# Second attention of a fused transformer kernel: GpSimd subtracts the row maxima for two of four head groups, ScalarE makes one wide exponential of each, and the instruction sequences of all engines are new

## The reference

```
x = x + cross_attention_0(layernorm(x), ctx)   # 16 heads of 8, causal, bf16 projections
x = x + ffn_0(layernorm(x))                    # shared expert + top-1 of 8 experts
x = x + cross_attention_1(layernorm(x), ctx, bias)   # 16 heads of 8, fp32, softmax over 128 keys
x = x + switchhead(layernorm(x))               # 8 heads; gated sums over 8 experts for values and outputs
```

## Time and profile before

| what | value |
|---|---|
| time, median of 3 runs | 1476.98 us (1474.19 to 1478.59) |
| time of the profiled execution | 1472.34 us |
| its span, first to last instruction | 1470.6 us |
| TensorE matmul busy | 1380.0 us, 94% |
| TensorE weight load busy | 931.6 us, 63% |
| VectorE busy | 1293.0 us, 88% |
| ScalarE busy | 1256.4 us, 85% |
| GpSimd busy | 863.4 us, 59% |

### The profile page before, as it was taken

The page is one execution under the profiler, slowest core; times in us unless marked ns, Lnnn a source line. Parts: engine busy times, 40 slices in busy tenths (PEclk is TensorE's granted clock), DMA queues, the critical chain, the costliest instruction groups (busy, mean ns, idle before and its releaser), DMA issues. The chain is left out here.

```text
span 1470.6 us, 34271 instructions
## 1 busy us (share of the span) xinstructions
PE 1380.0 (94%) x9428; PEld 931.6 (63%) x9585; DVE 1293.0 (88%) x5266; ACT 1256.4 (85%) x4426; POOL 863.4 (59%) x1345
## 2 busy tenths in 40 slices
PE   3477999999999999999999999999999999999998
PEld 2255666666666666666666666666666666666654
DVE  3666989999999999999989999999999999999886
ACT  2666889999888899998889999888999988899886
POOL 2122665665666566666665665656566566655567
PEclk8688999999999999999999999999999999999999
DMA  4520010000111100011110000111000011100000
GB/s 119 166 76 25 26 28 24 18 20 26 29 29 29 29 16 23 21 28 28 29 29 17 22 21 28 29 29 28 22 18 22 26 29 29 29 23 7 21 3 4
DMA packets 99966, 44.97 MB, mean 31 GB/s; under 512 B 21248, under 2 KB 99776, under 8 KB 99776
## 3 DMA queue, kind: packets, MB, share of 16 engines
q1 hardware_dynamic: 82560, 34.13, 8.3%
q10 hardware_dynamic: 17216, 8.65, 2.1%
HBM read 25.70 MB, written 8.52 MB: 23 GB/s over the span
## 5 line engine op out<-in xcount | busy, mean ns | idle before, releaser
L3422 POOL TENSOR_TENSOR accO<-accO,TE 128x512 f32<-128x512 f32 x192 | 247.2, 1287 | 184.6 <-DVE TE L2514 172.3
L1365 ACT ACTIVATE TE<-psC,gateO 128x128 f32<-128x128 f32 x1024 | 290.9, 369 | 46.0 <-PE psC L325 35.3
L1365 ACT ACTIVATE TE<-psC,gate 128x128 f32<-128x128 f32 x1024 | 298.8, 402 | 12.3 <-PE psC L325 6.8
L2514 DVE SCALAR_TENSOR_TENSOR TE<-psC,gateO,TE 128x128 f32<-128x128 f32 x1024 | 282.3, 340 | 12.0 <-PE psC L325 10.6
L2514 DVE SCALAR_TENSOR_TENSOR TE<-psC,gate,TE 128x128 f32<-128x128 f32 x1024 | 284.0, 339 | 9.0 <-ACT TE L1365 4.3
L325 PE MATMUL psC<-Oh,ch 128*128 128x512 f32 x512 | 269.5, 526 | 4.7 <-DVE TE L2514 4.2
L325 PE MATMUL psC<-Vh,xTh 128*128 128x512 f32 x512 | 267.0, 521 | 2.6 <-ACT PTC L1365 1.0
L3410 POOL TENSOR_TENSOR TE<-TE 128x256 f32<-128x256 f32 x256 | 192.1, 750 | 123.6 <-DVE TE L2514 120.3
L325 PE MATMUL psC<-Vh,xTl 128*128 128x512 f32 x512 | 202.0, 395 | 0.0
L325 PE MATMUL psC<-Oh,cl 128*128 128x512 f32 x512 | 201.8, 394 | 0.0
L325 PE MATMUL psC<-Ol,cb 128*128 128x512 bf16 x478 | 186.2, 390 | 0.0
(11 more groups left out here) (229 smaller groups left out, 3318.4 us busy)
## 6 DMA issues: line engine op xcount, KB each, us to landing
bdB<-k_rows SPq DMA_DIRECT2D x128, 64.0 KB, 2.3
k_rows<-Kc SPq DMA_DIRECT2D x96, 64.0 KB, 2.0
Qs<-Qc SPq DMA_DIRECT2D x96, 64.0 KB, 1.9
raw<-in_L_ffn_v_w ACTq DMA_DIRECT2D x8, 512.0 KB, 4.0
raw<-in_L_ffn_o_w ACTq DMA_DIRECT2D x8, 512.0 KB, 3.9
x_sb<-in_x SPq DMA_DIRECT2D x32, 64.0 KB, 2.1
ctx_sb<-in_ctx SPq DMA_DIRECT2D x32, 64.0 KB, 2.0
bias_sb<-in_mask_Bx1xSxS_ff SPq DMA_DIRECT2D x32, 64.0 KB, 1.9
```

The lines of the kernel that those rows point to most:

```text
L1365: return A.activation(o, i, func, **kw)
L2514: m = V.scalar_tensor_tensor(TE[:, i, e], psC[:, p, e * P:(e + 1) * P], gates[:, e:e + 1], TE[:, i, e], ALU.mult, ALU.add)
L3422: G.tensor_tensor(accO[:], TE[:, slot(b, H1)] if h == 1 else accO[:], TE[:, slot(b, H1 + h)], ALU.add).then_inc(o_fe, 1)
```

## The change

For head groups 2 and 3 of stage B the subtraction of the maximum leaves ScalarE. A new GpSimd step `b_below(b, t)` waits for `b_nm`, computes `nmB - PTB` for the 128x512 of the group in one TENSOR_TENSOR, with `nmB` read with a stride of zero along the keys, and counts the new semaphore `b_sub`. ScalarE's `b_exp` then waits for `b_sub` and makes one ACTIVATE of 128x512 with no bias. Groups 0 and 1 stay as they were.

```diff
@@ ScalarE @@
             def b_exp(b, t):
                 if b not in BATCHES:
                     return
-                act.wait_ge(b_nm, 4 * b + t + 1)
-                for j in range(NJ):
-                    m = copy(PTB[:, t, j], PTB[:, t, j], ACT.Exp, bias=nmB[:, t, j:j + 1], scale=-1.0)
-                m.then_inc(b_e, 1)
+                if t < 2:
+                    act.wait_ge(b_nm, 4 * b + t + 1)
+                    for j in range(NJ):
+                        m = copy(PTB[:, t, j], PTB[:, t, j], ACT.Exp, bias=nmB[:, t, j:j + 1], scale=-1.0)
+                    m.then_inc(b_e, 1)
+                    return
+                act.wait_ge(b_sub, 2 * b + t - 1)
+                copy(flat(PTB[:, t]), flat(PTB[:, t]), ACT.Exp).then_inc(b_e, 1)
@@ GpSimd @@
+            def b_below(b, t):
+                if b not in BATCHES:
+                    return
+                pool.wait_ge(b_nm, 4 * b + t + 1)
+                G.tensor_tensor(PTB[:, t], along(nmB[:, t, :], P), PTB[:, t], ALU.subtract).then_inc(b_sub, 1)
@@ GpSimd, period @@
...
+                outputs(i - 7, 6)
+                b_below(i - 4, 2)
+                b_below(i - 4, 3)
+                outputs(i - 7, 7)
...
```

More of the change, by code:

```diff
@@ L2534, in start @@
             def start():
+                ones()
                 a_stats(0, 0)
@@ L2714, in start @@
                 b_bias(2, 2)
+                c_choice(1, 0)
                 b_bias(2, 3)
@@ L2765, in start @@
                 a_top(3, 1)
+                c_share(1, 4)
                 a_top(3, 2)
@@ L2789, in start @@
                 outputs(0, 5)
+                c_share(1, 6)
                 a_max(4, 0)
                 b_bias(3, 0)
-                a_max(4, 1)
                 outputs(0, 6)
@@ L2871, in start @@
                 outputs(1, 3)
-                c_share(2, 5)
+                outputs(1, 4)
+                b_queries(4)
                 c_norm(3)
-                outputs(1, 4)
                 c_share(2, 6)
-                b_queries(4)
+                a_max(5, 0)
                 outputs(1, 5)
@@ L2964, in start @@
                 b_bias(5, 0)
-                a_max(6, 0)
                 outputs(2, 6)
@@ L2968, in start @@
                 b_bias(5, 2)
+                a_max(6, 0)
                 a_max(6, 1)
-                a_stats(7, 0)
+                c_xl_(4)
                 b_bias(5, 3)
-                c_xl_(4)
                 a_max(6, 2)
                 a_max(6, 3)
+                a_maxt(6, 0)
                 c_weights(3, 0)
-                a_maxt(6, 0)
                 a_maxt(6, 1)
                 outputs(2, 7)
+                c_choice(4, 0)
                 a_withmax(6)
@@ L3054, in period @@
                 b_bias(i - 1, 0)
+                a_max(i, 0)
                 outputs(i - 4, 6)
@@ L3057, in period @@
                 b_bias(i - 1, 2)
-                a_max(i, 0)
                 a_max(i, 1)
+                c_xl_(i - 2)
                 b_bias(i - 1, 3)
-                c_xl_(i - 2)
+                c_choice(i - 2, 0)
                 a_max(i, 2)
@@ L3457, in start @@
                 b_root(0)
-                a_masks(2)
+                b_below(0, 2)
+                b_below(0, 3)
                 a_causal(1, 0)
@@ L3470, in start @@
                 a_root(3)
-                a_masks(3)
+                b_below(1, 2)
+                b_below(1, 3)
                 a_causal(2, 0)
@@ L3657, in end @@
                 c_gates(B - 4, 2)
+                outputs(B - 5, 6)
+                b_below(B - 2, 2)
+                b_below(B - 2, 3)
                 outputs(B - 5, 7)
                 a_causal(B - 1, 0)
-                result(B - 5, 0)
                 a_causal(B - 1, 1)
                 a_causal(B - 1, 2)
+                result(B - 5, 0)
                 a_causal(B - 1, 3)
```

1170 lines of the change are left out of this document (585 added, 585 removed).

## The result

The change takes 1459.51 us, median of 4 runs (1457.87 to 1463.57), beside 1476.96 us (1474.19 to 1478.59) for the kernel before. The ratio is 0.9895, with a 95% interval of 0.9881 to 0.9909: faster by 1.05%, inside the range of the prediction and 4.5 us above its 1455. Timed beside each other a second time, the two kernels stood at 1460.36 and 1473.83, 13.5 us apart where the first pair has 17.5. The profiled execution took 1457.87 us, its span is 1456.1.

What follows compares the result with a forecast made beforehand. It took a nearly full TensorE to bound the long middle. Terms of 0.3 + 0.4 + 0.1 = 0.8 us, times 28 repetitions, gave 22.4 us off 1472.3, with 4.6 added for the median: 1455 us, range 1432 to 1490.

Steps and rivals of the forecast that it cites:

- the least: TensorE's matmul row: its idle time, 0.52 us a repetition, as the lower figure for what a perfect change could take.
- the most that a perfect change could take: TensorE's queue: the weight loads' waits for VectorE and ScalarE results, 2.0 us a repetition.
- five named waits: TensorE's weight loads, six repetitions: VectorE's `TE` 3.0 us, ScalarE's `PTA` 2.5, `PTB` 2.2, `TE` 2.0, VectorE's `nmA` 2.2.
- about a quarter: Share of the weight-load waits (2.0 us a repetition) that the matmul row shows as idle time (0.52).
- part 2: VectorE's order: one `c_share` product moves, an `outputs` group starts sooner, TensorE's wait there goes; 0.4 us, ends 0.26 and 0.5.
- Part 1: ScalarE's exponentials: wide ones save 1.3 us of its queue, of which TensorE gains 0.3 us a repetition, ends 0 and 1.1.
- the 0.1 us of `a_max`: VectorE: `a_max(b, 0)` goes ahead of `outputs(b, 6)`, easing the wait for `nmA`; 0.1 us a repetition, ends 0 and 0.37.
- Part 3: GpSimd: two added 128x512 instructions, 2.6 us a repetition, fit into 4.60 us idle before `outputs` 7; cost nothing.
- Part 4: The rest: SyncE's new order changes nothing at a DMA share of 0.09; start and end nothing, 5 us either way.
- A: All of TensorE's named waits go, 1.4 to 2.0 us a repetition: 1429 us; chance 0.12.
- B: No change: savings given back at stage B's first scores, behind the `Qs` transfer, or wide exponentials wait for GpSimd; 1477, chance 0.15.
- C: Slower: GpSimd's second `b_below` locks out small VectorE instructions, 1.29 us per repetition against 0.8 gained: 1491; chance 0.20.

Runs made afterwards that it cites:

- less_pe: The change without the product of low x by high y in stage C's scores, two matmuls per element: 1447.12 us, ratio 0.9814 to before.
- share_only: The kernel before with one VectorE instruction moved, `c_share` 5 from behind `outputs` 4 to ahead of `b_norm`: 1473.88 us, ratio 0.9991 to before.
- seq_only: The change with its new lists, but small exponentials for all four groups and no `b_below`: 1486.91 us, ratio 1.0085 to before.
- math_only: The kernel before with `b_below` and the wide exponentials alone, the order of calls otherwise as it was: 1480.51 us, ratio 1.0043 to before.
- math_steady: The kernel before with `b_below` and wide exponentials only for elements 3 to 27: 1473.51 us, ratio 0.9996 to before.
- sp_slack: The change with SyncE's next masks, bias and store issued before stage A's keys: 1454.10 us, ratio 0.9867 to before; timed again 1455.28, 0.9872.
- pool_more: The change with a third 128x512 TENSOR_TENSOR on GpSimd behind the second `b_below`: 1477.71 us, ratio 1.0021 to before.

## Why the prediction was right, and where it was not

**The bound.** That the middle decides and that TensorE is nearly full was right; less_pe shows it directly. The 0.70 us spacing of the earlier trace rows, and not the share of the weight loads, was the right reading. By the rule that the prediction gives from the Trainium skill, Perfetto Trace Analysis, Identifying the Most-Contended Engine, VectorE at 93% would have been the bound. Here the runs say otherwise: share_only freed VectorE of 1.0 us of it for 0.03, and less_pe freed TensorE of 0.46 for 0.45.

**The step that failed: from waits to time.** The prediction called the matmul row's 0.52 us "the least" and the weight-load waits' 2.0 us "the most that a perfect change could take". What was gained, 0.45 us, lies at the least. The change removed four of the five named waits, (3.0 + 2.5 + 2.2 + 2.2)/6 = 1.65 us a repetition, but the weight loads wait only 0.5 us less in all, since most of it came back at other places; that is close to the 0.45 gained. The working had a conversion (about a quarter) and used it for two terms, but not for part 2, which took 0.4 whole; with it part 2 is 0.12 and the sum 0.52, which gives about 1462 us for the whole. The idle time of the row was the better estimate, but no strict ceiling: seq_only's row has 0.37 us idle, and the change runs 0.8 us shorter than it with the same list on TensorE.

**Part 1, ScalarE, 0.3 us.** Mis-sized: 0.14 to 0.17 alone (math_only, math_steady). The exponential came as forecast, 0.52 us against 1.17; ScalarE ended at 37.49 busy, for 37.0.

**Part 2, VectorE's order, 0.4 us.** Fell as a separate term: 0.03 alone. The stretch of the small products that it wanted removed was removed. The rows of L2474, which answer to L2469 of the earlier trace rows:

```profile
L2474 DVE TENSOR_TENSOR best<-best,gsum x46: 161/175/644, 329.7 to 1266.5; 128x16 f32<-128x16 f32 x46
```

The median fell from 401 to 175 ns, and the wait of TensorE for VectorE's `TE` from 3.0 us in six to 0.7 in 24 repetitions. But what pays is the whole of the lists together with the wide exponential (0.31), not this move alone; the 0.1 us of `a_max` had no run of its own, and its wait for `nmA` is gone.

**Part 3, GpSimd, nothing.** Right. `b_below` was cheaper than its nearest row, 1.04 against 1.285 us, and ended 0.71 us ahead of ScalarE for group 2, where 0.24 was allowed for. A third instruction there (pool_more) costs 18 us, so the cost of nothing holds for two and not for GpSimd as such.

**Part 4, SyncE, nothing.** Wrong by about 5 us, by sp_slack beside the change. I read the share of the DMA engines (0.09) and not SyncE's own queue: each issue takes 0.6 us of it, and with them in a row the last `Qs` issue has no slack. Start and end were put at "nothing, and 5 us either way"; they came out 6.5 us better in one execution and 4.2 in another at the head, and 0.7 at the tail, at or beyond the edge of that.

So the 22.4 us forecast for the middle were 7.3, a third. The head and tail, at which the forecast put nothing, gave 7.2, and the profiled execution of before lay 4.6 us below its median where that of the change lay 1.6 below: that the total came out 17.5 us, near the forecast, was in good part luck. Of the signs named, the repetition of 41.7 us did not come (42.05), and the sign of being wrong, TensorE's waits again under other names, came in part.

**The rivals.** A (1429) did not come: its 1.4 to 2.0 us a repetition were three times what the row had idle, and the next wait was there, as its own counter-argument said. B named its place well: the long repetitions end at the first scores and `Qs`. C's mechanism is real at the place named (pool_more), and the change misses it by 0.25 us.

## What to carry to other kernels

Take the idle time of the matmul row (0.52 us here, for 0.45 gained), not the sum of named waits on the weight loads (2.0), as the first estimate of what a reordering can give TensorE, and check the sum of the terms against it. It is an estimate and no bound, as seq_only shows. Once TensorE is full, the next microseconds are in the tail of the distribution: compare repetitions one by one, and give the transfer that TensorE needs first an idle SyncE ahead of it. When engine A is relieved and queues are in fixed order, the gain appears only with an order written for the new times: test both halves alone before crediting either.

## What was not expected of the hardware

**Late issues of transfers.** On SyncE most issues take 0.6 to 0.7 us, now and then one 1.1 to 2.0. In the change, 300 to 1300 us, the trace has 560 issues. For 28 of them a 16 KB packet of the queue that the page calls "instruction" starts between 0.4 us before and 0.5 after the issue's start; 11 of these take over 0.9 us, and of the other 532 none does. The transfer view of 544.6 to 546.3 us, in which the second `Qs` issue of the long repetition above lasts 1.62 us:

```profile
DMA packets 148, 0.08 MB, mean 49 GB/s; under 512 B 18, under 2 KB 147, under 8 KB 147
...
q8 instruction: 1, 0.02, 4.3%
```

In the kernel before only 2 of 21 such issues were late, and 2 of 531 without such a packet. So the packet goes with lateness but is neither enough for it nor always there; that it is the cause is argued, and no run here moved those packets.

**The same operation at two prices.** TENSOR_TENSOR of 128x512 on GpSimd takes 1.29 us with two full inputs (`accO`) and 1.04 when one is read with a stride of zero (`b_below`), over 47 instructions between 1.034 and 1.057.

**An issue from GpSimd** took 0.62 us of its queue, like those of SyncE, and left the clean repetition as it was, 42.04 us, with VectorE busy for 39.12 us of it instead of 38.87 in sp_slack.
